# Two attention layers on one core: x read in blocks of 32 and turned by VectorE, with new orders of work

## The chip, the cores and the metric

One core of a Trainium2 chip runs the whole program, one launch. The metric is device microseconds of that core. Shown are the median of three runs and one execution taken by the profiler. TensorE (PE in the profile) does the products, VectorE (DVE), ScalarE (ACT) and GpSimd (POOL) the work between them, SyncE (SP) issues the DMAs. Each engine takes its instructions in the order in which they were written, and waits on semaphores.

## The reference

128 graphs of 128 nodes with 384 features go through two attention layers of 12 heads of 32, each with a residual and a layer norm. All arithmetic is f32.

```
# layer 0, for each graph
q, k, v = x @ Wq0.T, x @ Wk0.T, x @ Wv0.T + bv0
s  = q_h @ k_h.T * 384**-0.5 + 2 * adj          # rows that are all zero give p = 0
x1 = layernorm(x + concat(softmax(s) @ v_h) @ Wo0.T + bo0)
# layer 1
q, k, v = x1 @ Wq1 + bq1, x1 @ Wk1 + bk1, x1 @ Wv1 + bv1
s   = q_h @ k_h.T * 32**-0.5 + beta * adj, and -9e15 where adj <= 0
out = layernorm(x1 + concat(softmax(s) @ v_h))
```

## The kernel before

The graphs are taken in 64 pairs. Everything between x and the output stays in SBUF and PSUM. A product with f32 precision is split: each operand is kept as a high part (`_hi`, f32r) and a low part (`_lo`, the difference), and `split_product` adds three products, hi x hi, hi x lo and lo x hi, over three chunks of 128 features: nine matmuls. A `project_qk` makes one 128-feature chunk of q or k for both graphs of a pair (nine matmuls of 256 columns; six such calls a layer), `project_v` and `project_out0` a graph's v or output projection (nine of 384 columns). `scores` and `attend` are 24 small matmuls each, `transpose_x`, `transpose_x1` and `transpose_out1` three transposes of 128 x 128 through PSUM.

`iterations` runs the body of each engine for n = -2 to 68, the middle of it as a hardware loop of two bodies a turn. In a body, `n` is the current pair and `m1`, `m2`, `p1`, `p2` the pairs before and after it: the body is a software pipeline, in which layer 0 of the current pair, layer 1 of pairs two to five back and the first projections of the next stand side by side. The order of the calls in a body is written out by hand for each engine, and the five orders are independent: what an engine finds at its head it waits for.

`r_bank` is a ring of four PSUM banks for all results but the scores. Who uses which bank follows from the list `RING_USERS`, in TensorE's order; `BANK` is the place in it modulo four. `s_bank` are four banks for the scores of both layers.

The way of x before: `load_x` (line 231) brings a graph as 128 rows of 384 into `x_in`, two buffers; `transpose_x` (line 333) transposes it on TensorE into a bank of the ring; `high_xT` (line 499, ScalarE) copies it to `xT_hi`; `low_xT` (line 720, VectorE, through `low_part`, line 715) subtracts that from the bank into `xT_lo`. `residual0` (line 865, GpSimd) adds `bo` to `x_in` into `x_bo`, which `add_residual0` (line 657, VectorE) adds to the output projection.

The probabilities of layer 0: `negate` (line 678, VectorE) takes the scores out of PSUM with their maxima, `exps` (line 574, ScalarE) the exponentials. Meanwhile `fold_scores0` (line 892, GpSimd) adds the negated scores in halves, which `abs_max` (line 739, VectorE) sums, to find rows that are all zero. `inverse_sums0` (line 775, VectorE) makes the factor of each row and head, `normalise0` (line 919, GpSimd) multiplies, `flip_probs` (line 700, VectorE) transposes in blocks of 32 into `flip0`, and `spread_probs` (line 283, SyncE) brings the blocks to their places in `probT` with four DMAs. The fold's scratch lies in `flip0` as well, and it says so by a wait:

```
fold_a = flip0[:, 0:H * N // 2].rearrange("p (h k) -> p h k", h=H)
...
pool.wait_ge(probT_loaded[0], q.count(16 * NB, g, 0))
```

Other work of GpSimd is `make_bias1` (line 877: three steps that make the mask and bias of layer 1), `inverse_std` (line 848: three small steps of a layer norm), `late_x1` (line 903) and `residual1` (line 912).

At the start SyncE loads x of pair 0, then the weights by `load_weights` (line 262), one DMA each, the biases and the adjacency; GpSimd's first step behind its constants is line 951, which needs the biases bq and bk. `high_weights` (ScalarE) and `low_weights` split the weights.

Of the kernel before, what the change touches and what calls it, by code (L numbers as in the profile page):

```python
# [20 lines left out]
F32 = mybir.dt.float32  # L21
# [10 lines left out]
NB = N // HD  # L32
PAIRS = NG // 2
# [20 lines left out]
RING_USERS = ["g0_4", "v1_1", "v0_1", "x1t0", "g0_5", "x1t1", "xt0", "pv0_0",  # L54
              "pv1_0", "xt1", "g1_0", "g1_1", "ot_0", "g0_0", "g1_2", "g1_3",
              "g1_4", "wo_0", "pv1_1", "pv0_1", "g0_1", "g1_5", "g0_2", "g0_3",
              "ot_1", "wo_1", "v0_0", "v1_0"]
RING = 4
assert len(RING_USERS) % RING == 0
# [52 lines left out]
def build(nc, x, adj, wts, bv0, bo0, bq1, bk1, bv1, beta, out):  # L112

    with ExitStack() as ctx:
# [26 lines left out]
        x_in = [sb(f"x_in{b}", [P, 2, D]) for b in range(2)]  # L141
# [9 lines left out]

        xT_hi, xT_lo = sb("xT_hi", [P, C, G2], F32R), sb("xT_lo", [P, C, G2], F32R)
# [33 lines left out]
        x_loaded, adj0_loaded, adj1_loaded = sems("x_loaded"), sems("adj0_loaded"), sem("adj1_loaded")  # L186
# [8 lines left out]
        xt_done, x1t_done = sem("xt_done"), sem("x1t_done")  # L195
# [34 lines left out]
        def _(sp):  # L230
            def load_x(q):
                if q.valid():
                    b = q.parity

                    sp.wait_ge(xt_done, q.plus(-2).count(1, 1, 1))
                    sp.wait_ge(x_bo_done, q.plus(-2).count(1, 1, 1))
                    for g in range(2):
                        sp.dma_start(x_in[b][:, g, :], x[bass.ds(2 * q.index() + g, 1)].rearrange("g (j a) d -> a j (g d)", j=NB)
                                     ).then_inc(x_loaded[b], 16)
# [25 lines left out]


            load_x(Pair(0, 0))
            load_weights(WQ0)
            load_weights(WK0)
            for layer, b_ in enumerate((bv0, bv1)):  # L270
                sp.dma_start(bv_row[layer][:], b_.partition_broadcast(P)).then_inc(bv_loaded, 16)
            load_weights(WV0)
# [21 lines left out]
            def body(r, off):  # L294
                n = Pair(r, off)
                m5, m4, m3, m2, m1, p1, p2 = (n.plus(-5), n.plus(-4), n.plus(-3), n.plus(-2), n.plus(-1), n.plus(1), n.plus(2))

                spread_probs(1, m4, 1)
                if not is_peeled(r, off, -1):
                    load_adj0(p1)  # L300
                spread_probs(0, m1, 1)
                load_adj1(m2)
                store(m5, 1)
                spread_probs(1, m3, 0)
                spread_probs(0, n, 0)
                if not is_peeled(r, off, -2):
                    load_x(p2)
                store(m4, 0)
# [8 lines left out]
        def _(pe):  # L317

            read = [(xt_lo_done, 0, 0, 0, 0)] * 4
# [12 lines left out]

            def transpose_x(q, g, r):
                if q.valid():
                    pe.wait_ge(*last_read(read, BANK[f"xt{g}"], r))
                    read[BANK[f"xt{g}"]] = (xt_lo_done, q.off, 1, g, 1)
                    pe.wait_ge(x_loaded[q.parity], q.loads(2))
                    for c in range(C):
                        mm = pe.transpose(ring(f"xt{g}")[:, c * P:(c + 1) * P],  # L339
                                          x_in[q.parity][:, g, c * P:(c + 1) * P], ident[:])  # L340
                    mm.then_inc(xt_done, 1)
# [110 lines left out]
            def body(r, off):  # L452
                n = Pair(r, off)
                m4, m3, m2, m1, p1, p2 = (n.plus(-4), n.plus(-3), n.plus(-2), n.plus(-1), n.plus(1), n.plus(2))

                scores(0, n, 0, r)
                transpose_x(p1, 1, r)
                project_qk(1, m2, 0, r)
                project_qk(1, m2, 1, r)
# [33 lines left out]
        def _(act):  # L493
# [97 lines left out]
            def body(r, off):  # L591
# [6 lines left out]
                if is_peeled(r, off, -1):  # L598
                    high_weights(WO0)
# [383 lines left out]
```

## Time and profile before

| | |
|---|---|
| median of three runs | 2124.54 us (2122.32 to 2125.64) |
| profiled execution | 2125.58 us, span 2123.8 us from the first to the last instruction |
| mean granted clock of TensorE | 0.985 |
| busy share of the span | TensorE 96%, ScalarE 89%, VectorE 85%, GpSimd 77% |
| data moved by DMA | 273 MB on SyncE's queue in 225,360 packets |

Busy is the time in which an engine had an instruction running. "Idle before, releaser" is the time it stood still ahead of an instruction, and the line whose semaphore ended that. TensorE's matmuls overlap, so their spacing, not their length, is what one costs.

### The profile page before, as it was taken

The numbers are of one execution on the slowest core, as the hardware profiler recorded it, in microseconds if no ns is written. First come the engines' busy times: TensorE is split into PE (matmuls) and PEld (weight loads), VectorE is DVE, ScalarE is ACT, GpSimd is POOL, SyncE is SP. The second block draws the span as 40 slices with busy tenths as digits, with TensorE's granted clock in tenths as the row PEclk, the third lists the DMA queues.
The fourth block names the chain that finished last, engine by engine and source line by source line (L and its number), as shares of the span: only waits on it lengthen the run. The fifth ranks groups of instructions, "written<-read, shape, count | busy, mean of one in ns | idle before, by whom it ended". The sixth has DMA issues, their size and how long they took to land.

```text
span 2123.8 us, 86803 instructions
## 1 busy us (share of the span) xinstructions
PE 2046.2 (96%) x23808; PEld 1923.4 (91%) x23808; DVE 1814.6 (85%) x8324; ACT 1888.1 (89%) x7816; POOL 1643.1 (77%) x2187
## 2 busy tenths in 40 slices
PE   5799999999999999999999999999999999999984
PEld 5799999999999999999999999999999999999973
DVE  3578888888988988888988988988989888888875
ACT  4489999999999999999999999999999999999975
POOL 2667877888877878878878888888888888787774
PEclk9899999999999999999999999999999999999997
DMA  4245555555555555555555555555555555555554
GB/s 134 58 101 136 135 130 136 132 128 135 132 136 127 133 139 124 136 135 128 138 134 130 137 133 130 141 131 126 139 132 129 134 132 136 127 132 139 118 122 107
DMA packets 225439, 274.19 MB, mean 129 GB/s; under 512 B 25681, under 2 KB 225361, under 8 KB 225361
## 3 DMA queue, kind: packets, MB, share of 16 engines
q1 hardware_dynamic: 225360, 273.26, 53.5%
q8 instruction: 36, 0.59, 0.1%
q14 instruction: 43, 0.34, 0.1%
HBM read 46.67 MB, written 25.17 MB: 34 GB/s over the span
## 4 chain that ended last, share of the span: by engine, by line
PE 87%; POOL 4%; issue 3%; DMA 3%; SPq 2%; DVE 1%; ACT 0%; POOLq 0%; DVEq 0%
PE r_bank L356 22%; PE r_bank L357 21%; PE r_bank L358 21%; PE s_bank L407 10%; PE r_bank L423 8%; DMA prob0T<-flip 2%; PE r_bank L339 2%; PE r_bank L349 2%; PE r_bank L435 2%; SPq L291 1%; POOL prob L924 1%; POOL flip L897 1%; DVE flip L711 1%; POOL w_lo L845 0%; DMA stage<-in_L_gnn_Wv_dram 0%
## 5 line engine op out<-in xcount | busy, mean ns | idle before, releaser
L586 ACT ACTIVATE prob<-neg_s,heads 128x128 f32<-128x128 f32 x3072 | 1191.1, 394 | 18.7 <-DVE flip L711 11.1
L586 ACT ACTIVATION_READ_ACCUMULATOR prob<-neg_s,heads 128x1 f32 x3072 | 594.2, 193 | 0.0
L924 POOL TENSOR_TENSOR prob<-prob,heads 128x512 f32<-128x512 f32 x384 | 389.2, 1042 | 98.7 <-DVE heads L783 98.7
L897 POOL TENSOR_TENSOR flip<-neg_s 128x768 f32<-128x768 f32 x128 | 235.8, 1842 | 186.6 <-DMA prob0T<-flip 171.3
L356 PE MATMUL r_bank<-xT_hi,w_hi 128*128 128x256 f32 x1152 | 357.9, 311 | 14.6 <-DVE xT_lo L717 13.6
L695 DVE CUSTOM_DVE_ANT_0 neg_s<-s_bank,bias 128x128 f32<-128x128 f32 x1536 | 333.5, 286 | 20.6 <-PE s_bank L407 18.9
L695 DVE CUSTOM_DVE_ANT_0 neg_s<-s_bank,adj 128x128 f32<-128x128 f32 x1536 | 333.8, 286 | 2.3 <-PE s_bank L407 1.6
L356 PE MATMUL r_bank<-x1T_hi,w_hi 128*128 128x256 f32 x1152 | 330.8, 287 | 3.8 <-DVE x1T_lo L717 3.8
L358 PE MATMUL r_bank<-xT_hi,w_lo 128*128 128x256 f32 x1152 | 327.9, 285 | 0.0
L357 PE MATMUL r_bank<-xT_lo,w_hi 128*128 128x256 f32 x1152 | 327.9, 285 | 0.0
L357 PE MATMUL r_bank<-x1T_lo,w_hi 128*128 128x256 f32 x1152 | 325.0, 282 | 0.0
L358 PE MATMUL r_bank<-x1T_hi,w_lo 128*128 128x256 f32 x1152 | 324.8, 282 | 0.0
L356 PEld LDWEIGHTS r_bank<-xT_hi,w_hi 128*128 128x128 f32 x1152 | 219.4, 190 | 43.6 <-DVE xT_lo L717 14.6
L695 DVE DVE_READ_ACCUMULATOR2_ANT heads<- 128x1 f32 x3072 | 255.7, 83 | 0.1
L711 DVE STREAM_TRANSPOSE flip<-prob 128x1536 f32<-128x1536 f32 x128 | 227.4, 1777 | 20.6 <-POOL prob L924 19.3
L711 DVE STREAM_TRANSPOSE stage<-prob 128x1536 f32<-128x1536 f32 x128 | 225.4, 1761 | 7.5 <-DMA prob1T<-stage 7.5
L356 PEld LDWEIGHTS r_bank<-x1T_hi,w_hi 128*128 128x128 f32 x1152 | 217.7, 189 | 5.3 <-issue 5.1
L357 PEld LDWEIGHTS r_bank<-xT_lo,w_hi 128*128 128x128 f32 x1152 | 220.8, 192 | 0.0
L358 PEld LDWEIGHTS r_bank<-xT_hi,w_lo 128*128 128x128 f32 x1152 | 220.3, 191 | 0.0
L357 PEld LDWEIGHTS r_bank<-x1T_lo,w_hi 128*128 128x128 f32 x1152 | 218.0, 189 | 0.0
L358 PEld LDWEIGHTS r_bank<-x1T_hi,w_lo 128*128 128x128 f32 x1152 | 217.7, 189 | 0.0
L858 POOL TENSOR_TENSOR norm<-norm,neg_half 128x1 f32<-128x1 f32 x256 | 144.0, 563 | 21.3
(85 smaller groups left out, 5493.6 us busy)
## 6 DMA issues: line engine op xcount, KB each, us to landing
prob0T<-flip SPq DMA_DIRECT2D x512, 192.0 KB, 3.6
prob1T<-stage SPq DMA_DIRECT2D x512, 192.0 KB, 3.6
x_in<-in_x_dram SPq DMA_DIRECT2D x128, 192.0 KB, 3.3
out_dram<-y SPq DMA_DIRECT2D x128, 192.0 KB, 2.3
adj<-in_adj_dram SPq DMA_DIRECT2D x256, 64.0 KB, 2.7
prob<-in_L_gnn_Wq_dram SPq DMA_DIRECT2D x1, 576.0 KB, 5.6
prob0T<-in_L_gnn_Wk_dram SPq DMA_DIRECT2D x1, 576.0 KB, 6.5
stage<-in_L_gnn_Wv_dram SPq DMA_DIRECT2D x1, 576.0 KB, 7.6
```

Of the source, the lines that this page charges most:

```text
L339: mm = pe.transpose(ring(f"xt{g}")[:, c * P:(c + 1) * P], x_in[q.parity][:, g, c * P:(c + 1) * P], ident[:])
L356: pe.matmul(dst, a_hi(c), b_hi(c), start=(c == 0), stop=False)
L357: pe.matmul(dst, a_hi(c), b_lo(c), start=False, stop=False)
L358: mm = pe.matmul(dst, a_lo(c), b_hi(c), start=False, stop=(c == C - 1))
L407: mm = pe.matmul(s_bank[j][:, c * N:(c + 1) * N], qT[layer][q.parity][rows, c, m], kT[layer][q.parity][rows, c, m], start=True, stop=True)
L423: mm = pe.matmul(ring(name)[HD * j:HD * (j + 1), c * N:(c + 1) * N], v[layer][q.parity][:, g, f], probT[layer][:, :, HC * c + j, :], start ...
L586: act.activation(prob[layer][:, h, :], neg_s[layer][:, h, :], ACT.Exp, bias=neg_max[layer][:, h:h + 1], scale=-1.0, accum_out=row_sum[laye ...
L695: dve.tensor_tensor_reduce(neg_s[layer][:, h, :], s_bank[b][:, (h // HC) * N:(h // HC + 1) * N], (adj0, bias1)[layer][q.parity][:, g, :], ...
L711: dve.transpose(flip[layer].rearrange("p (j h b) -> p h j b", j=NB, h=H), prob[layer][:].rearrange("p h (j a) -> p h j a", j=NB)).then_inc ...
L858: pool.tensor_tensor(rstd[layer][g][:], var_eps[layer][g][:], neg_half[:], ALU.pow).then_inc(rstd_steps[layer], 1)
L897: pool.tensor_tensor(fold_a, neg_s[0][:, :, 0:N // 2], neg_s[0][:, :, N // 2:N], ALU.add).then_inc(fold_steps, 1)
L924: pool.tensor_tensor(prob[0][:, hs, :], prob[0][:, hs, :], inv_sum0[:, hs].unsqueeze(2).to_broadcast([P, HC, N]), ALU.mult).then_inc(probn ...
```

## The change

x is read twice. `load_q` (SyncE) reads both graphs of a pair with four DMAs into `x_q`, a single buffer: partitions 32 i to 32 i + 31 take features 96 i to 96 i + 95 of the rows, 32 rows to a block, so its contiguous pieces are 96 features, 384 bytes. `flip_x` (VectorE) transposes `x_q` in blocks of 32 x 32 into `xT`; row 32 i + b of chunk c is then feature 96 i + 32 c + b. The weights that meet it (WQ0, WK0, WV0) are loaded in the same order of features by `load_rows`, four DMAs each, those of WQ0 and WK0 from ScalarE's queue. `high_xT` (ScalarE) reads `xT` in place of a PSUM bank, and `low_xT` is GpSimd's now; both read `xT` in the order of the nodes that the columns of `xT_hi` have, a step of 32 elements within runs of four. `load_x` reads x once more, straight into `x_bo`, where `residual0` adds `bo` in place. The six transposes of a pair and their two users of the ring are gone; the list has 26 names, no longer a multiple of four. All five orders of calls are new, and `load_q`, `load_adj0` and `flip_x` work two pairs ahead.

```
+            def load_q(q):
+                if q.valid():
+                    sp.wait_ge(xflip_done, q.count(1, 0, 0))
+                    for i in range(NB):
+                        sp.dma_start(x_q[HD * i:HD * (i + 1), :, :],
+                                     x[bass.ds(2 * q.index(), 2)].rearrange("g (j a) d -> a (g j) d", j=NB)[:, :, QD * i:QD * (i + 1)]
+                                     ).then_inc(xq_loaded, 16)
             def load_x(q):
-                    sp.wait_ge(xt_done, q.plus(-2).count(1, 1, 1))
-                    sp.wait_ge(x_bo_done, q.plus(-2).count(1, 1, 1))
+                    sp.wait_ge(y0_done, q.plus(-2).count(1, 1, 1))
...
+            load_q(Pair(0, 0))
+            load_rows(WV0)
...
+                if not is_peeled(r, off, -2):
+                    load_q(p2)
                 spread_probs(0, m1, 1)
                 store(m5, 1)
                 spread_probs(1, m3, 0)
+                if not is_peeled(r, off, -2):
+                    load_adj0(p2)
+                store(m4, 0)
                 spread_probs(0, n, 0)
+                load_adj1(m1)
+                load_x(n)
+                spread_probs(1, m3, 1)
...
-            def transpose_x(q, g, r):
...
             def high_xT(q, g):
-                    act.wait_ge(xt_done, q.count(1, g, 1))
+                    act.wait_ge(xflip_done, q.count(1, g, 1))
...
+                    act.activation(xT_hi[:, :, g * N:(g + 1) * N].rearrange("p c (a j) -> p c a j", j=NB), rows_xT(g), ACT.Copy).then_inc(xt_hi_done, 1)
...
+            def flip_x(q, g):
+                if q.valid():
+                    dve.wait_ge(xq_loaded, q.count(8 * NB, 1, 8 * NB))
+                    dve.wait_ge(xt_lo_done, q.plus(-1).count(1, g, 1))
+                    dve.transpose(xT[:, :, g * N:(g + 1) * N].rearrange("p c (j a) -> p c j a", j=NB),
+                                  x_q[:, g * NB:(g + 1) * NB, :].rearrange("p j (c b) -> p c j b", c=C)
+                                  ).then_inc(xflip_done, 1)
...
+            def low_xT(q, g):
+                if q.valid():
+                    pool.wait_ge(xt_hi_done, q.count(1, g, 1))
...
+                    pool.tensor_tensor(*(t.rearrange("p c (a j) -> p c a j", j=NB) if i != 1 else t.rearrange("p c (j a) -> p c a j", j=NB)
+                                        for i, t in enumerate((xT_lo[:, :, m], xT[:, :, m], xT_hi[:, :, m].bitcast(F32)))), ALU.subtract
+                                      ).then_inc(xt_lo_done, 1)
```

The new orders of the engines on which most turns (TensorE, VectorE, GpSimd; each call stands for one line of the body):

```
TensorE: project_qk(0, n, 4); scores(1, m3, 0); attend(1, m4, 0); transpose_x1(m2, 1); project_qk(0, n, 5);
  transpose_out1(m4, 0); attend(0, m1, 0); scores(0, n, 0); project_v(0, n, 1); project_qk(1, m2, 0);
  project_v(1, m2, 0); project_qk(1, m2, 1); project_out0(m1, 0); project_qk(1, m2, 2); project_qk(1, m2, 3);
  attend(1, m4, 1); scores(1, m3, 1); transpose_out1(m4, 1); project_qk(1, m2, 4); project_qk(1, m2, 5);
  attend(0, m1, 1); scores(0, n, 1); project_qk(0, p1, 0); project_out0(m1, 1); project_qk(0, p1, 1);
  project_qk(0, p1, 2); project_v(0, p1, 0); project_qk(0, p1, 3); transpose_x1(m1, 0); project_v(1, m2, 1)
VectorE: flip_probs(1, m3, 0); norm_input0(m1, 0); negate(1, m3, 1); flip_x(p2, 0); attention_out1(m4, 1);
  low_o0T(m1, 1); abs_max(n, 0); inverse_sums0(n, 0); negate(0, n, 1); add_residual0(m1, 1); flip_probs(0, n, 0);
  values_out0(p1, 0); norm_input1(m4, 1); norm_input0(m1, 1); flip_probs(1, m3, 1); inverse_sums1(m3, 1);
  low_x1T(m1, 0); negate(1, m2, 0); low_x1T(m1, 1); attention_out1(m3, 0); flip_x(p2, 1); low_o0T(n, 0);
  abs_max(n, 1); inverse_sums0(n, 1); negate(0, p1, 0); values_out0(p1, 1); flip_probs(0, n, 1);
  add_residual0(n, 0); norm_input1(m3, 0); inverse_sums1(m2, 0)
GpSimd: make_bias1(m2, 0); inverse_std(1, m4, 0); low_xT(p1, 0); low_xT(p1, 1); fold_scores0(n, 0);
  inverse_std(0, m1, 0); normalise0(n, 0); late_x1(m2, 0); residual1(m4, 1); make_bias1(m2, 1);
  inverse_std(0, m1, 1); inverse_std(1, m4, 1); late_x1(m2, 1); fold_scores0(n, 1); residual1(m3, 0);
  normalise0(n, 1); residual0(n)
```

## Rows read from the trace of the kernel before

**Rows 1.** Stretch, busy us: PE, PEld, DVE, ACT, POOL (instructions); clock, DMA share, GB/s.

```profile
400.00:1000.00 600.00, 600.00 (x7071) 567.14 (x7070) 537.75 (x2474) 556.95 (x2321) 485.29 (x646) 1.00 0.56 133
```

**Rows 2.** Timeline of TensorE, scores of layer 0 (start, length, instruction).

```profile
214.88 0.95 PE L407 MATMUL s_bank<-k0T,q0T 32*128 32x128 f32 x24
...
1921.41 1.26 PE L407 MATMUL s_bank<-k0T,q0T 32*128 32x128 f32 x24
```

**Rows 3.** Waits of GpSimd: in total, times, longest.

```profile
POOL flip L897 <- DMA prob0T<-flip: 171.3, 125, 8.2
```

**Rows 4.** Timeline of GpSimd, two turns; idle before and releaser in brackets.

```profile
1000.79 1.85 POOL L897 TENSOR_TENSOR flip<-neg_s 128x768 f32<-128x768 f32 x1 [1.30 <-DMA prob0T<-flip]
...
1005.24 3.04 POOL L924 TENSOR_TENSOR prob<-prob,heads 128x512 f32<-128x512 f32 x3 [1.51 <-DVE heads L783]
...
1016.79 1.84 POOL L897 TENSOR_TENSOR flip<-neg_s 128x768 f32<-128x768 f32 x1 [1.04 <-DMA prob0T<-flip]
...
1019.81 0.22 POOL L855 TENSOR_SCALAR norm<-norm 128x1 f32<-128x1 f32 x1
...
1021.12 3.04 POOL L924 TENSOR_TENSOR prob<-prob,heads 128x512 f32<-128x512 f32 x3
...
1025.22 0.66 POOL L885 TENSOR_SCALAR mask<-adj 128x128 f32<-128x128 f32 x1
...
1027.35 0.24 POOL L855 TENSOR_SCALAR norm<-norm 128x1 f32<-128x1 f32 x1
...
1032.19 1.86 POOL L897 TENSOR_TENSOR flip<-neg_s 128x768 f32<-128x768 f32 x1 [1.10 <-DMA prob0T<-flip]
```

**Rows 5.** Timeline of VectorE in the second of these turns.

```profile
1019.76 0.55 DVE L744 TENSOR_REDUCE heads<-flip 128x12 f32<-128x384 f32 x1 [0.45 <-POOL flip L900]
...
1024.28 1.78 DVE L711 STREAM_TRANSPOSE flip<-prob 128x1536 f32<-128x1536 f32 x1 [0.29 <-POOL prob L924]
```

**Rows 6.** Timeline of SyncE in that turn, the four issues of a spread.

```profile
1026.09 3.00 SPq L291 DMA_DIRECT2D prob0T<-flip  x4
```

**Rows 7.** Timeline of TensorE around the two transposes of x.

```profile
1004.02 0.49 PE L339 MATMUL r_bank<-ident,x_in 128*128 128x128 f32 x3
1004.44 0.86 PE L423 MATMUL r_bank<-prob0T,v 128*32 128x128 f32 x24
...
1006.77 0.55 PE L339 MATMUL r_bank<-ident,x_in 128*128 128x128 f32 x3
1007.07 0.36 PE L356 MATMUL r_bank<-x1T_hi,w_hi 128*128 128x256 f32 x1
1007.27 0.28 PE L357 MATMUL r_bank<-x1T_lo,w_hi 128*128 128x256 f32 x1
1007.39 0.28 PE L358 MATMUL r_bank<-x1T_hi,w_lo 128*128 128x256 f32 x1
```

**Rows 8.** Groups of instructions by shape: count, busy, mean ns, idle before.

```profile
L711 DVE STREAM_TRANSPOSE flip<-prob 128x1536 f32<-128x1536 f32 x128 | 227.4, 1777 | 20.6 <-POOL prob L924 19.3
...
L717 DVE TENSOR_TENSOR xT_lo<-r_bank,xT_hi 128x384 fp32r<-128x384 f32 x128 | 71.3, 558 | 35.0 <-ACT xT_hi L505 33.4
...
L565 ACT ACTIVATE x<-y,norm 128x384 f32<-128x384 f32 x128 | 90.2, 704 | 26.6 <-POOL norm L862 26.5
...
L505 ACT ACTIVATE xT_hi<-r_bank 128x384 fp32r<-128x384 f32 x128 | 62.5, 489 | 16.9 <-PE r_bank L339 14.6
...
L874 POOL TENSOR_TENSOR x_bo<-x_in,bo_row 128x384 f32<-128x384 f32 x128 | 127.4, 1017 | 0.0
```

**Rows 9.** DMA issues: count, KB each, median us to landing.

```profile
adj<-in_adj_dram SPq DMA_DIRECT2D x256, 64.0 KB, 2.7
```

**Rows 10.** Timelines of SyncE, TensorE and GpSimd at the start.

```profile
9.03 0.56 SPq L278 DMA_DIRECT2D bqk<-in_L_gnn_bk_dram  x1
...
15.54 0.55 PE L356 MATMUL r_bank<-xT_hi,w_hi 128*128 128x256 f32 x1 [9.15 <-DVE xT_lo L717]
...
16.96 0.26 POOL L951 TENSOR_SCALAR bq1s<-bqk 128x3 f32<-128x3 f32 x1 [15.30 <-DMA bqk<-in_L_gnn_bk_dram]
```

More of the change, by code:

```diff
@@ L139, in build @@
         neg_half = sb("neg_half", [P, 1])
-        x_in = [sb(f"x_in{b}", [P, 2, D]) for b in range(2)]
+        x_q = sb("x_q", [P, 2 * NB, QD])
         x_bo = [sb(f"x_bo{b}", [P, 2, D]) for b in range(2)]
@@ L264, in load_weights, with load_rows @@
                              ).then_inc(w_loaded[i], 16)
-            load_x(Pair(0, 0))
-            load_weights(WQ0)
-            load_weights(WK0)
+            def load_rows(i):
+                for k in range(NB):
+                    sp.dma_start(w_stage[i][HD * k:HD * (k + 1), :, :],
+                                 wts[i][QD * k:QD * (k + 1), :].rearrange("(c b) o -> b c o", c=C)).then_inc(w_loaded[i], 16)
+            load_q(Pair(0, 0))
+            load_rows(WV0)
             for layer, b_ in enumerate((bv0, bv1)):
                 sp.dma_start(bv_row[layer][:], b_.partition_broadcast(P)).then_inc(bv_loaded, 16)
-            load_weights(WV0)
             load_adj0(Pair(0, 0))
@@ L493, in _, with load_rows, rows_xT @@
         def _(act):
+            def load_rows(i):
+                for k in range(NB):
+                    act.dma_start(w_stage[i][HD * k:HD * (k + 1), :, :],
+                                  wts[i][QD * k:QD * (k + 1), :].rearrange("(c b) o -> b c o", c=C)).then_inc(w_loaded[i], 16)
+            load_rows(WQ0)
+            load_rows(WK0)
             def high_weights(*which):
                 for i in which:
-                    act.wait_ge(w_loaded[i], 16)
+                    act.wait_ge(w_loaded[i], 16 * (NB if i in (WV0, WQ0, WK0) else 1))
                     act.activation(w_hi[i][:], w_stage[i], ACT.Copy).then_inc(w_hi_done[i], 1)
+            def rows_xT(g):
+                return xT[:, :, g * N:(g + 1) * N].rearrange("p c (j a) -> p c a j", j=NB)
             def high_xT(q, g):
                 if q.valid():
-                    act.wait_ge(xt_done, q.count(1, g, 1))
+                    act.wait_ge(xflip_done, q.count(1, g, 1))
                     if g == 0:
@@ new lines, in body @@
+                qk_out(1, m1, 0, r)
+                exps(1, m2, 0, 6, 8)
+                values_out1(m1, 0)
+                exps(1, m2, 0, 8, 10)
+                high_xT(p2, 1)
+                if is_peeled(r, off, -2):
+                    high_weights(WO0)
+                exps(1, m2, 0, 10, 12)
+                exps(0, p1, 0, 0, 2)
+                qk_out(1, m1, 1, r)
+                exps(0, p1, 0, 2, 4)
+                qk_out(1, m1, 2, r)
+                qk_out(1, m1, 3, r)
+                out1T_out(m3, 1)
```

244 lines of the change are left out of this document (106 added, 138 removed).

## The prediction

> **What bounds the kernel now.** I read the page's busy shares first (the table above). They average over filling, steady state and draining, so next comes the steady state alone, the windows view from 400 to 1000 us [rows 1]: TensorE is busy 600.00 of 600.00 us, ScalarE 556.95, VectorE 537.75, GpSimd 485.29, at a granted clock of 1.00 (its level of 2.4 GHz). TensorE has no gap at all there. Third, the length of a pair: the first layer's scores of graph 12 start at 214.88 and those of graph 120 at 1921.41, 54 pairs later [rows 2], so a pair takes 1706.53 / 54 = 31.60 us. 64 pairs of that are 2022 us; the other 101 us of the 2123.8 us span are filling and draining.
>
> The fourth view is there because a full TensorE hides what is second. In the waits of GpSimd, the fold of layer 0 (line 897) waits 125 times for the transfer prob0T<-flip [rows 3]: nearly every one of 128. So there is a ring of work that is almost as long as TensorE's pair. flip0 is a single buffer and also the scratch of the fold: fold, abs_max, inverse, normalise, flip, four DMAs, landing, next fold. Two turns of it, one per graph, start at 1000.79, 1016.79 and 1032.19 [rows 4]: 16.00 + 15.40 = 31.40 us. The reader is to see in [rows 4 to 6] that the second turn has nothing slack in it: fold 1016.79, maximum of its sums 1019.76, normalise 1021.12 to 1024.16, flip 1024.28 to 1026.06, four DMAs issued 1026.09 to 1029.09, next fold 1032.19. The first turn is 0.6 us longer. Two turns at the shorter length are 30.80 us. The change touches no step of this ring but where its steps stand in the queues, so whatever TensorE is relieved of, a pair will not go below about 30.8.
>
> **The change part by part.**
>
> TensorE loses two triples of transposes per pair. In [rows 7] the first starts at 1004.02 and the next instruction at 1004.44, 0.42 us; the second runs from 1006.77 to 1007.07, 0.30 us. Together 0.72 us a pair, which are on the path that sets the end. The order of what is left is new too. TensorE's body had seven runs of short matmuls (transposes, scores, attend) between the wide products; the new one has five. Behind a short run the first wide product holds the next one back: 1007.07 to 1007.27, and 0.12 us from there to the third [rows 7], so two runs fewer could give 0.2 more; but attend now stands right behind a projection twice, which the trace of before has nowhere, and that may take back as much as 0.2. I take 31.60 - 0.72 = 30.88 us for TensorE, ends 30.7 and 31.1.
>
> VectorE loses low_xT, 558 ns twice [rows 8], and gains flip_x, a stream transpose of 384 elements per partition. The trace has it only at 1536 elements, 1777 ns. A quarter of that is 0.44, the lower end; the upper end is the 0.56 that VectorE needs today for a pass over 384 elements. I take 0.55, for an instruction has a fixed part: VectorE's work stays as it is, 28.3 us a pair (537.75 / 600 of 31.60).
>
> ScalarE's high_xT reads SBUF instead of PSUM, in a permuted order. Lower end the 489 ns of today, upper end the 704 ns of a ScalarE pass over 384 elements in SBUF with its own scale and bias [rows 8]. It is nearest to the first, a plain copy, so 0.5. ScalarE is at 29.3 us a pair and stays there, at most 29.8: no bound, but 95% of the new pair.
>
> GpSimd gains low_xT twice a pair, a subtraction of 384 elements from SBUF. GpSimd's waits for others in the two turns of [rows 4] are 1.51, 1.04 and 1.10 us, so it is occupied 31.40 - 3.65 = 27.75 us a pair. The nearest row has the same size and contiguous operands: 1017 ns [rows 8], 1.10 with the gap to the next. The new one reads one of three operands with a step of 32 elements, inner runs of four. No GpSimd row has such a step; the other end is the fold of 768 elements, 1.84 us, as if each element cost double. I take 1.1, since two of the three streams stay as they are. GpSimd: 27.75 + 2.2 = 29.95, and 0.3 that it must still wait between its fold and normalise (that gap, filled by inverse_std today, is 1019.81 to 1021.12, 1.3 us, and in one turn the new order puts residual1 there, 1.0 us). 30.25 us: under TensorE, but with hardly a gap. At 1.84 us it is 31.9 with the gaps.
>
> The Trainium skill's page GPSIMD Engine Reference, section Performance pitfalls for Q7 kernels, speaks against this move: a read from SBUF whose step is over 8 bytes costs about 2.9 cycles an element instead of 1.9. By that low_xT would be an estimated 1.34 us and GpSimd 30.9 us a pair, level with TensorE; no run here shows it yet.
>
> The ring's window for GpSimd counts as well. From the end of normalise to the next fold the flip and its transfer take 1024.16 to 1032.19, 8.0 us. In one turn GpSimd now has residual0, make_bias1, inverse_std and both low_xT there: 2.0 + 2.1 + 1.3 + 2.2 = 7.6 us (residual0 is twice line 874 [rows 8]; bias 1025.22 to 1027.35 and inverse 1019.81 to 1021.12 [rows 4]). In the other late_x1 twice, residual1, make_bias1 and inverse_std twice: about 7.9. Both fit, by 0.4 and 0.1 us; the ring stays near 30.8.
>
> SyncE issues four more DMAs a pair (x_q) and reads x twice. Four flip issues take 3.0 us [rows 6], so four x_q issues about 3 us of a queue that now spends 24 issues on 31.6 us. The x_q DMAs stand ahead of the spread of the second graph's probabilities, released by flip_x of the pair before, which stands six steps ahead of that spread's flip in VectorE's order. What must land after them is on the ring. 96 KB in rows of 384 bytes each: nearest are the 64 KB adjacency blocks in rows of 512 bytes, 2.7 us [rows 9], and the flip's 192 KB, whose last part lands 3.1 us after the four issues end [rows 4, 6]. They should be gone before the spread starts; each microsecond that they are not lengthens one turn by as much.
>
> The start gets longer. Before, TensorE's products begin at 15.54, and GpSimd has no part in that; its own first work waits until 16.96 for bk, issued at 9.03 [rows 10]. Now low_xT of pair 0 stands behind that wait. As the 17th DMA of SyncE's queue in place of the 14th (four x_q for two x, four WV0 for one, less WQ0 and WK0, which go to ScalarE's queue), at 0.6 us an issue, bk comes at 17 to 19, then two low_xT, so TensorE starts at 19 to 22: 3.5 to 6.5 us later, I take 5. The draining follows the same chain; I cost it at nothing, ends -4 and +4.
>
> **The sum.** The pair is the longest of TensorE 30.88, the ring 30.80, GpSimd 30.25; as three in-order queues that meet within 0.6 us will not mesh without loss I add 0.1, an estimate: 31.0. About 60 pairs run at that rate, since the first few, which the ring sets, do not: 60 x (31.60 - 31.00) = 36 us. Less 5 at the start: the span becomes 2123.8 - 31 = 2092.8. The profiled execution took 2125.58, 1.8 beyond its span, so 2094.6; the median of the runs shown, 2124.54, is 1.0 below the profiled one. I forecast 2094 us. Below 0.2%, 4.2 us, a measurement of this kernel can't tell a difference.
>
> **The rivals.**
>
> *GpSimd becomes the bound.* If low_xT costs 1.84 us, GpSimd's pair is 31.9: 60 x 0.3 + 5 = 23 us more, 2147. For it: the only unmeasured access pattern falls on the engine that the ring passes through. Against it: two of three streams are contiguous. The point where it decides: 60 x (31.60 - P) = 5 gives P = 31.52, that is 27.75 + 0.3 + 2c = 31.52, c = 1.74 us with the gap, about 1.65 in the row. This is the case on the slower side, chance 0.14.
>
> *The ring holds the pair.* The extra transfers (1024 rows of x_q a pair) make the spread land later, or VectorE comes late to abs_max or flip because something ahead of it in the new order waits for TensorE. Half a microsecond a turn on one of the two turns gives 31.4 instead of 30.8: 60 x 0.2 - 5 = 7 us gained, 2117; a whole one gives 31.8, 2141. For it: the first turn is already 0.6 us longer than the second, so the queues do cost it something today. Against it: the spreads land some microseconds before attend wants them. Chance 0.17 for 2109 to 2121, of which a fifth lies within the 0.2%; another 0.06 for no change at all.
>
> The Trainium skill's page DMA: Bandwidth & Descriptors, section Specifications, is on this rival's side: under 512 bytes a transfer does not run at line rate, for the engine reads, modifies and writes. The shortest data rows of before are the adjacency's 512 bytes, so the trace can't say what 384 cost.
>
> *The change doesn't do what it says*, in that TensorE's idle time grows by what the transposes gave back: then the pair stays at 31.6 and the start's 5 us make 2129. It is in the chances of no change and slower, 0.03.
>
> **How the numbers follow.** The forecast, 2078 to 2108, has 0.60. Faster by over 0.2% is that and most of the ring's case: 0.74. Within 0.2%: 0.10. Slower: 0.16. The range that leaves two in ten out runs from 2076 (the pair at the ring's 30.8, start +3.5, draining -4) to 2122.
>
> **What would show it.** Right: the scores' spacing at about 31.0 us with TensorE still full; VectorE's stream transpose of 384 at about 0.55 us; low_xT near 1.1; waits of the fold for prob0T<-flip much smaller, since GpSimd comes to it late. Wrong: low_xT at 1.6 or more and GpSimd without any wait; attend (line 423) waiting for prob0T; spreads that land over 4.5 us after issue; TensorE's first product after 22 us.

## The result: slower, 2145.57 us

The changed kernel takes 2145.57 us (median of 4 runs, 2144.28 to 2147.01) against 2123.56 for the kernel before (4 runs, 2122.32 to 2125.64): a ratio of 1.0107, with a 95% interval of 1.0091 to 1.0122. The forecast was 2094, with a range from 2076 to 2122. The profiled execution of the changed kernel took 2144.28 us with a span of 2142.0.

### The profile after

The steady state of the kernel after, in the same windows view as [rows 1]:

```profile
400.00:1000.00 600.00, 598.67 (x6940) 559.17 (x6938) 536.34 (x2469) 566.87 (x2314) 527.05 (x684) 1.00 0.59 145
```

By its share TensorE is as full as before, at the same granted clock of 1.00, but it gets through 6940 matmuls in place of 7071. Six transposes fewer in each of the 19 pairs of that stretch explain 6 x 19 = 114 of the 131; the rest fits pairs that come a little more slowly. GpSimd is up by 42 us and ScalarE by 10; VectorE is where it was.

The length of a pair comes from TensorE's timeline. The first two of these rows are the first and the last graph of the kernel before, start, length and instruction of the scores of layer 0 (graphs 12 and 120 are in [rows 2]):

```profile
27.32 0.95 PE L407 MATMUL s_bank<-k0T,q0T 32*128 32x128 f32 x24
...
2034.31 1.67 PE L407 MATMUL s_bank<-k0T,q0T 32*128 32x128 f32 x24
```

The kernel after, graphs 0, 12, 120 and 127:

```profile
32.34 0.95 PE L407 MATMUL s_bank<-k0T,q0T 32*128 32x128 f32 x24 [0.47 <-ACT k0T L547]
...
214.97 0.95 PE L407 MATMUL s_bank<-k0T,q0T 32*128 32x128 f32 x24
...
1928.93 1.26 PE L407 MATMUL s_bank<-k0T,q0T 32*128 32x128 f32 x24
...
2045.64 0.95 PE L407 MATMUL s_bank<-k0T,q0T 32*128 32x128 f32 x24
```

The subtraction tells where the 18.2 us of span went. The start costs 5.0 (27.32 to 32.34), but filling gives it back: graph 12 starts at 214.97, as before. The 54 pairs from graph 12 to graph 120 take 1713.96 us, 31.74 a pair in place of 31.60: 7.4 us. The last graphs, 120 to 127, take 116.7 in place of 112.9: 3.8 us. From there to the end it is 96.4 in place of 89.5: 6.9 us. So the pair, which was to become 0.6 us shorter, is 0.14 longer.

The groups of the parts that are new or moved (count, busy, mean ns, idle before), answering to [rows 8]:

```profile
L917 POOL TENSOR_TENSOR flip<-neg_s 128x768 f32<-128x768 f32 x128 | 233.6, 1825 | 76.5 <-DMA prob0T<-flip 75.5
...
L908 POOL TENSOR_TENSOR xT_lo<-xT,xT_hi 128x384 fp32r<-128x384 f32 x128 | 153.3, 1220 | 16.1 <-ACT xT_hi L514 16.1
L514 ACT ACTIVATE xT_hi<-xT 128x384 fp32r<-128x384 f32 x128 | 118.5, 928 | 12.0 <-PE r_bank L358 8.2 <-DVE xT L733 2.1 <-issue 1.3
L733 DVE STREAM_TRANSPOSE xT<-x_q 128x384 f32<-128x384 f32 x128 | 73.0, 571 | 15.3 <-POOL xT_lo L908 9.8 <-DMA x_q<-in_x_dram 5.5
```

flip_x takes 571 ns (0.55 was taken), low_xT 1220 (1.1), high_xT 928 (0.5, with 0.704 as the upper end).

GpSimd's waits (in total, times, longest) answer to [rows 3]:

```profile
POOL flip L917 <- DMA prob0T<-flip: 75.5, 115, 8.3
```

The total is less than half of 171.3, which looks like the forecast, but the count says otherwise: in 115 of 128 turns the fold still waits for the spread of the graph before. GpSimd comes to it later, because low_xT now fills the time; the spread still lands last. Here are three turns in GpSimd's timeline, in the place of [rows 4]:

```profile
1008.22 1.84 POOL L917 TENSOR_TENSOR flip<-neg_s 128x768 f32<-128x768 f32 x1
...
1021.20 2.39 POOL L908 TENSOR_TENSOR xT_lo<-xT,xT_hi 128x384 fp32r<-128x384 f32 x2
1023.97 1.82 POOL L917 TENSOR_TENSOR flip<-neg_s 128x768 f32<-128x768 f32 x1 [0.39 <-DMA prob0T<-flip]
...
1039.70 1.83 POOL L917 TENSOR_TENSOR flip<-neg_s 128x768 f32<-128x768 f32 x1 [0.37 <-DMA prob0T<-flip]
...
1055.99 1.82 POOL L917 TENSOR_TENSOR flip<-neg_s 128x768 f32<-128x768 f32 x1 [0.91 <-DMA prob0T<-flip]
```

The turns take 15.75, 15.73 and 16.29 us, and in each the wait of the fold is what closes it. One step of the ring starts late for a reason that can be seen. VectorE's flip of the turn that begins at 1023.97, and SyncE's queue behind it:

```profile
1031.43 1.78 DVE L720 STREAM_TRANSPOSE flip<-prob 128x1536 f32<-128x1536 f32 x1
```

```profile
1031.21 1.33 SPq L252 DMA_DIRECT2D adj<-in_adj_dram  x2
1032.75 0.65 SPq L265 DMA_DIRECT2D out_dram<-y  x1
1033.57 3.04 SPq L300 DMA_DIRECT2D prob0T<-flip  x4
```

The flip ends at 1033.21. SyncE is then still issuing the store that stands ahead of the spread (to 1033.40), and the first of the four DMAs goes out at 1033.57, 0.36 us late. Averaged over the turns of graphs 20 to 115, a turn from fold to fold takes 15.79 us for the first graph of a pair and 15.91 for the second, 31.70 together; in the kernel before 15.51 and 16.07, 31.58. There is one fold per graph, so these sums are the length of a pair whatever sets it. What tells more is each step inside a turn, and SyncE's delay behind the flip above all: it averages 0.03 us for the first graph and 0.59 for the second in the kernel before, and 0.39 and 0.03 in the kernel after. The long turn of [rows 4], which begins at 1000.79, shows where the 0.59 came from. VectorE and SyncE of the kernel before, in that turn:

```profile
1008.40 1.78 DVE L711 STREAM_TRANSPOSE flip<-prob 128x1536 f32<-128x1536 f32 x1
```

```profile
1009.29 1.33 SPq L246 DMA_DIRECT2D adj<-in_adj_dram  x2
1010.72 3.05 SPq L291 DMA_DIRECT2D prob0T<-flip  x4
```

The flip ends at 1010.18, but the adjacency's load stands ahead of the spread and is being issued until 1010.62. The new order moved this load, with a store, ahead of the other graph's spread, and the delay moved with it.

That leaves a question: how can TensorE wait for anything if it is busy 598.67 of 600 us? Its timeline around two scores (after each, the first wide product that follows):

```profile
1009.79 1.08 PE L407 MATMUL s_bank<-k0T,q0T 32*128 32x128 f32 x24
1010.80 0.45 PE L356 MATMUL r_bank<-w_hi,xT_hi 128*128 128x384 f32 x1
...
1025.10 0.95 PE L407 MATMUL s_bank<-k0T,q0T 32*128 32x128 f32 x24
1026.04 0.38 PE L356 MATMUL r_bank<-xT_hi,w_hi 128*128 128x256 f32 x1
```

The first step takes 1.01 us and shows no gap, because the scores are drawn longer. In other pairs the same step takes 0.88. If for each of the 30 stretches of a pair, from the start of one block of products to the start of the next, the 5th percentile over 48 pairs of the steady state is taken, they add up to 30.99 us; the means add up to 31.70. Taking the 5th percentile as the work and the rest as waits, the kernel before has 31.40 us of work in a pair and 0.2 of waits. So TensorE's own work is 0.4 us shorter than before, and its waits grew from 0.2 to 0.7 us. These stand at four places: after the scores of each graph of layer 0 (0.20 and 0.25 us a pair on average), and around the projection of the attention's output (0.12 and 0.07).

### The profile page after: what moved, and what is told of

The parts are those of the page before. It is cut to its first block, busy times and chain, and to the rows that moved or that the text cites. A ratio compares the mean times of both kernels' runs of the same rounds, so it can differ in the third digit from the quotient of the medians.

```text
span 2142.0 us, 86733 instructions
## 1 busy us (share of the span) xinstructions
PE 2045.4 (95%) x23424; PEld 1905.7 (89%) x23424; DVE 1818.7 (85%) x8324; ACT 1928.7 (90%) x7816; POOL 1789.1 (84%) x2315
## 4 chain that ended last, share of the span: by engine, by line
PE 62%; POOL 17%; issue 9%; DVE 4%; DMA 4%; SPq 2%; ACT 1%; POOLq 1%; DVEq 0%; ACTq 0%
PE r_bank L356 16%; PE r_bank L358 15%; PE r_bank L357 15%; PE s_bank L407 8%; PE r_bank L423 6%; POOL flip L917 4%; DMA prob0T<-flip 4%; POOL prob L944 2%; POOL norm L868 2%; PE r_bank L435 2%; PE r_bank L349 2%; SPq L300 1%; POOL x_late L929 1%; DVE neg_s L704 1%; POOL flip L920 1%
## 5 line engine op out<-in xcount | busy, mean ns | idle before, releaser
L356 PE MATMUL r_bank<-xT_hi,w_hi 128*128 128x256 f32 x1152 | 339.4, 295 | 29.8 <-POOL xT_lo L908 23.7
L908 POOL TENSOR_TENSOR xT_lo<-xT,xT_hi 128x384 fp32r<-128x384 f32 x128 | 153.3, 1220 | 16.1 <-ACT xT_hi L514 16.1
```

Of the source, the lines that this page charges most:

```text
L356: pe.matmul(dst, a_hi(c), b_hi(c), start=(c == 0), stop=False)
L908: pool.tensor_tensor(*(t.rearrange("p c (a j) -> p c a j", j=NB) if i != 1 else t.rearrange("p c (j a) -> p c a j", j=NB) for i, t in enum ...
```

## The experiments

Four theories of where the gain went: **A**, the ring of fold, maximum, normalise, flip, spread and next fold is as long as a pair and holds it; **B**, ScalarE and GpSimd are too full with high_xT at 928 and low_xT at 1220 ns; **C**, the traffic of x_q delays the spreads; **D**, VectorE's new order makes TensorE wait for banks whatever the ring does.

**own_scratch: the ring opened.** The fold's scratch leaves flip0 for a third of stage that is free by then, so the fold waits for the maximum of the graph before instead of the landing of its spread.

```
-        fold_a = flip0[:, 0:H * N // 2].rearrange("p (h k) -> p h k", h=H)
-        fold_b = flip0[:, H * N // 2:H * N * 3 // 4].rearrange("p (h k) -> p h k", h=H)
+        fold_a = stage[:, H * N:H * N * 3 // 2].rearrange("p (h k) -> p h k", h=H)
+        fold_b = fold_a[:, :, 0:N // 4]
...
-                    pool.wait_ge(probT_loaded[0], q.count(16 * NB, g, 0))
+                    pool.wait_ge(absmax_steps, q.count(2, g, 0))
...
```

> The changed kernel with the scratch of the fold moved out of flip0 into the free third of stage, so that the fold no longer waits for the landing of the spread before it. Theory A, the ring (fold, maximum, normalise, flip, four DMAs, landing, fold) sets the pair of 31.74 us: the ring is open now, TensorE becomes the bound at its stall-free 31.0 us, 60 x 0.7 = 42 us less than 2145, about 2103, and the hidden stalls of TensorE behind scores go. Theory B, ScalarE (94% busy, high_xT at 0.93 us) with GpSimd is simply full and each call waits for another: the pair stays above 31.5, 2130 to 2146. Theory C, the extra DMA traffic of x_q: the spreads still land late, but nothing but attend waits for them: also about 2105, so this run alone does not tell A from C.

2113.70 us, 0.995 of before [0.9933, 0.9966]; the pair is 31.30. The fold no longer waits for a DMA at all. 32 us come back by one change of place of a scratch buffer: theory A has most of it. It is 11 us short of the 2103 that A gave, for one wait of TensorE is left: in each of 48 pairs of the steady state project_qk(0, p1, 0) starts 0.13 us after the end of VectorE's attention_out1.

**contig: ScalarE and GpSimd relieved, the ring closed.** flip_x writes its result with a step, so that high_xT and low_xT read contiguous rows.

```
...
-                    dve.transpose(xT[:, :, g * N:(g + 1) * N].rearrange("p c (j a) -> p c j a", j=NB),
+                    dve.transpose(xT[:, :, g * N:(g + 1) * N].rearrange("p c (a j) -> p c j a", j=NB),
...
```

> The changed kernel with flip_x writing its blocks into the final order of the columns (a step of 4 elements on VectorE's side), so that high_xT and low_xT read and write contiguously. Theory A (ring): high_xT falls to about 0.5 us and low_xT to 1.02, but the ring keeps its length: pair 31.5 to 31.7, 2132 to 2145. Theory B (ScalarE and GpSimd full): 0.8 us a pair off ScalarE and 0.4 off GpSimd give the pair 31.1 or so, about 2107. Theory C: no change, 2145. flip_x itself may take longer than 0.57 us with the step.

2145.64 us, 1.0101 [1.0084, 1.0118]; the pair is 31.78. The groups (count, busy, mean ns, idle before) and the steady state of this kernel:

```profile
L908 POOL TENSOR_TENSOR xT_lo<-xT,xT_hi 128x384 fp32r<-128x384 f32 x128 | 126.6, 1011 | 15.3 <-ACT xT_hi L514 15.3
L733 DVE STREAM_TRANSPOSE xT<-x_q 128x384 f32<-128x384 f32 x128 | 113.4, 887 | 12.4 <-POOL xT_lo L908 7.5 <-DMA x_q<-in_x_dram 4.9
L514 ACT ACTIVATE xT_hi<-xT 128x384 fp32r<-128x384 f32 x128 | 66.3, 519 | 13.5 <-PE r_bank L358 8.4 <-DVE xT L733 2.6 <-issue 1.3
```

```profile
400.00:1000.00 600.00, 594.10 (x6935) 555.25 (x6934) 541.03 (x2458) 556.54 (x2308) 519.06 (x682) 1.00 0.59 145
```

high_xT and low_xT become as cheap as forecast, ScalarE is back at the 557 us of [rows 1], and the pair doesn't move. But flip_x now takes 887 ns in place of 571 on VectorE, so this run alone would leave theory B a way out. own_scratch closes it: there ScalarE and GpSimd have the same work as in the kernel after, and the pair is 31.30. Theory B falls.

**xq_short: the traffic taken away.** After the first pair each x_q DMA reads one of its eight blocks.

```
+                    blocks = slice(0, 2 * NB if is_peeled(q.r, q.off, 0) else 1)
...
-                        sp.dma_start(x_q[HD * i:HD * (i + 1), :, :],
+                        sp.dma_start(x_q[HD * i:HD * (i + 1), blocks, :],
```

> The changed kernel with the four x_q DMAs of each pair behind the first reading one of eight blocks, so 128 rows of 384 bytes a pair instead of 1024 (what is left out is seven eighths of the read of x for layer 0's products; the steps and waits stay). Theory C: the spreads land 0.2 to 0.3 us earlier, two turns a pair, pair about 31.2, about 2113. Theory A: a little of that, 31.5 to 31.7, 2130 to 2143. Theory B: 2143 to 2147.

2143.87 us, 1.0099 [1.0082, 1.0116]. The DMA share of the stretch goes from 0.59 to 0.54, the turns stay at 15.81 and 15.89, and the spreads land no earlier: the last part 3.98 and 4.35 us after its issue began, in place of 3.98 and 4.37. Theory C falls, as far as the bytes go; the four issues are still there.

**before_scratch: the ring opened in the kernel before.** The same edit in the other kernel.

```
...
-                    pool.wait_ge(probT_loaded[0], q.count(16 * NB, g, 0))
+                    pool.wait_ge(absmax_steps, q.count(2, g, 0))
...
```

> The kernel before with the same own scratch of the fold, as a control. Theory A says that TensorE, which had no gap in steady state, is the bound there and the ring (31.40 of 31.60 us) is not: the pair stays at 31.55 to 31.60, only the filling, where the ring ruled for some eight graphs, gets shorter: 2095 to 2122. If the ring had set the pair of the kernel before too, its pair would fall below 31.4.

2118.58 us, 0.9976 [0.9966, 0.9985]. The pair stays at 31.60 (1706.4 us for the 54); the gain lies in filling, where graph 12 starts at 209.5 in place of 214.9, and in draining. So in the kernel before TensorE, with its own order, holds the 31.60 with the ring open as well, and the closed ring, though its fold waits in 125 of 128 turns, isn't what sets the pair. How much shorter than 31.60 that ring would turn by itself, this run doesn't show.

**sp_order: one known delay of the ring taken out.** The spread of the first graph goes ahead of the adjacency's load and the store in SyncE's order; the ring stays closed.

```
                 spread_probs(1, m3, 0)
+                spread_probs(0, n, 0)
                 if not is_peeled(r, off, -2):
                     load_adj0(p2)
                 store(m4, 0)
-                spread_probs(0, n, 0)
```

> The changed kernel with one move in SyncE's order: the spread of the first graph's probabilities stands ahead of load_adj0 and the store, which in the changed kernel delay its first issue by 0.39 us behind the flip. The ring stays closed. Theory A (the ring sets the pair): the pair falls by about that, 31.74 to 31.35, 54 pairs of it are 21 us, about 2122. Theory B (the ring was only one of several that meet; what is taken out of one place turns up as a wait at the next of its steps): the 0.39 us goes into later waits, pair 31.6 to 31.75, 2138 to 2146.

2130.71 us, 1.0029 [1.0019, 1.0039]; the pair is 31.48. VectorE's flip and SyncE's queue in a turn of this kernel:

```profile
1026.77 1.78 DVE L720 STREAM_TRANSPOSE flip<-prob 128x1536 f32<-128x1536 f32 x1
```

```profile
1028.58 3.03 SPq L300 DMA_DIRECT2D prob0T<-flip  x4
1031.88 1.41 SPq L252 DMA_DIRECT2D adj<-in_adj_dram  x2
```

The flip ends at 1028.55 and the spread goes out at 1028.58. Of the 0.36 us that left the first graph's turn the pair got back 0.26, which is as a ring that sets the pair would have it, but for 0.1. GpSimd's waits show where the 0.1 went:

```profile
POOL flip L917 <- DMA prob0T<-flip: 60.2, 72, 7.9
```

The fold waits in 72 turns, no longer in 115: at the end of the first graph's turn GpSimd now comes to it behind the landing, 3.10 us after the end of the last issue in place of 3.00. There GpSimd's own order ends the turn. (Theory B of the expectation is that of several bounds that meet, not the B from above; a little of it is true.)

**dve_first: only VectorE's order.** attention_out1, which frees a bank for TensorE, goes ahead of flip_x; the ring stays closed.

```
-                flip_x(p2, 0)
                 attention_out1(m4, 1)
+                flip_x(p2, 0)
```

> The changed kernel, ring closed, with one swap in VectorE's order: attention_out1(m4, 1) ahead of flip_x(p2, 0). TensorE's project_qk(0, p1, 0) reuses the bank that attention_out1 reads, and stalls there about 0.25 us a pair. Theory A (the ring sets the pair of 31.74): the stall is only where TensorE's waiting for the ring shows, so the pair stays within 0.1 us, 2139 to 2147. Theory D (this wait of TensorE on VectorE is the bound): the flip's 0.5 us go from the path, pair about 31.3, 2115 to 2122.

2145.06 us, 1.0092 [1.0075, 1.0109], a pair of 31.79. The wait after the scores of the second graph shrinks (from 1.16 to 1.06 us on average to the next block) and that after the first graph's grows (from 1.07 to 1.17): the sum is the ring's. Theory D falls as the cause.

**scratch_dve: both.** The ring opened and attention_out1 first.

```
+        fold_a = stage[:, H * N:H * N * 3 // 2].rearrange("p (h k) -> p h k", h=H)
...
-                flip_x(p2, 0)
                 attention_out1(m4, 1)
+                flip_x(p2, 0)
...
```

> The same swap on the changed kernel with the fold's own scratch (pair 31.30, where the stall ahead of project_qk(0, p1, 0) is the one left). Theory A with D behind it: ring open and attention_out1 0.5 us earlier, TensorE reaches its stall-free 31.05: 54 x 0.25 = 13 us less than 2114, about 2100. If the stall is a wait for low_xT on GpSimd instead, no change: 2112 to 2116.

2109.03 us, 0.9924 [0.9908, 0.9941], a pair of 31.20. It is the best of all kernels here, and beats the kernel before by 16 us; theory A with D behind it had 2100. Its steady state, and the scores of two graphs with what follows:

```profile
400.00:1000.00 600.00, 600.00 (x7010) 563.93 (x7004) 537.31 (x2502) 579.26 (x2345) 534.78 (x692) 1.00 0.60 147
```

```profile
1007.35 0.95 PE L407 MATMUL s_bank<-k0T,q0T 32*128 32x128 f32 x24
1008.23 0.39 PE L356 MATMUL r_bank<-xT_hi,w_hi 128*128 128x256 f32 x1
...
1023.19 0.95 PE L407 MATMUL s_bank<-k0T,q0T 32*128 32x128 f32 x24
1024.07 0.44 PE L356 MATMUL r_bank<-w_hi,xT_hi 128*128 128x384 f32 x1
```

In both the step is 0.88 us, where the rows of the kernel after have 0.94 behind the second graph's scores and 1.01 behind the first's. In every second pair the step behind the second graph's is still longer, 1.24 us. With the ring open the order of VectorE is worth 0.1 us a pair; with the ring closed it was worth nothing.

**scratch_dve_sp: sp_order on top.** The spread of the first graph ahead of load and store, ring open.

```
...
                 spread_probs(1, m3, 0)
+                spread_probs(0, n, 0)
...
```

> As scratch_dve, with the spread of the first graph ahead of load_adj0 and the store in SyncE's order as well. With the ring open SyncE's 0.39 us are on no ring; both theories: as scratch_dve within 4 us. If it gains as much as it did with the ring closed (15 us), the spread's landing is still on the path, by way of flip or attend.

2109.76 us, 0.9929 [0.9912, 0.9946], a pair of 31.21. What gave 0.26 us a pair with the ring closed gives nothing when it is open. That is the strongest evidence that the ring passed SyncE's delay on to TensorE.

**contig_scratch: the contiguous reads with the ring open.**

```
+        fold_a = stage[:, H * N:H * N * 3 // 2].rearrange("p (h k) -> p h k", h=H)
...
+                    dve.transpose(xT[:, :, g * N:(g + 1) * N].rearrange("p c (a j) -> p c j a", j=NB),
...
```

> The changed kernel with the fold's own scratch and the contiguous high_xT and low_xT together. With the ring open the pair was 31.30, TensorE 31.05 without stalls, ScalarE 96% busy. Theory A1 (behind the ring, ScalarE is next): 0.8 us less of ScalarE brings the pair to TensorE's 31.05, about 2100. Theory A2 (what is left is TensorE's one stall ahead of project_qk(0, p1, 0), which waits for VectorE's attention_out1): flip_x takes 0.89 in place of 0.57 us on VectorE, so the stall grows and the pair is 31.3 to 31.5, 2113 to 2125.

2127.09 us, 1.0011 [1.0001, 1.002], a pair of 31.54, which is 0.24 longer than own_scratch, though ScalarE and GpSimd do less. TensorE's waits (in total, times, longest) name what is late:

```profile
PE r_bank L356 <- DVE y L771: 16.1, 54, 0.4
```

flip_x at 887 ns stands ahead of attention_out1 (L771) on VectorE, and the bank that this frees comes later: project_qk(0, p1, 0) starts 0.13 us after the end of attention_out1 in each of 48 pairs, as in own_scratch, and its step behind the scores is 1.42 us in place of 1.17, which is all of the 0.24. The 0.3 us on VectorE at that place are worth more than the 0.8 on ScalarE and 0.4 on GpSimd that they save. The time lies 2 us above what theory A2 had.

**old_order, old_order_scratch and old28: the new way of x in the old orders.** To tell whether the orders took the gain, x_q, flip_x and high_xT were put into the five bodies of the kernel before, without transpose_x. In the first two low_xT stays on VectorE and the list of banks loses xt0 and xt1; old_order_scratch opens the ring as well. old28 has the ring open, keeps the old list of 28 and has low_xT on GpSimd.

VectorE's body of before, and TensorE's:

```
             def body(r, off):
...
+                flip_x(p1, 1)
                 low_x1T(m2, 1)
...
                 values_out0(p1, 1)
+                flip_x(p2, 0)
                 low_x1T(m1, 0)
...
-                transpose_x(p1, 1, r)
...
-                transpose_x(p2, 0, r)
```

GpSimd's body in old28:

```
+                low_xT(p1, 1)
                 late_x1(m3, 0)
...
                 normalise0(n, 1)
+                low_xT(p2, 0)
```

> The new way of x in the orders of the kernel before: transpose_x left out of TensorE's order, flip_x on VectorE where it is needed, low_xT on VectorE at its old places (reading xT in SBUF), load_q at the place of load_x and load_x one pair later, the ring list without its two names. So GpSimd has its old work. Theory A: TensorE loses 0.72 us a pair but the closed ring, 31.4 us in the kernel before, keeps the pair at 31.2 to 31.5: 2105 to 2122. If the new orders were needed for the change, some queue jams and the pair is over 31.6: 2125 or more.

> The same with the fold's own scratch. Theory A: the ring is open, TensorE has 30.9 us of work, VectorE 29.4, ScalarE 30.2: pair 30.9 to 31.2, and the filling gains as it did in the kernel before with own scratch: 2080 to 2100. If VectorE's 1.1 us more or the closer reuse of the ring's banks is what counts, 31.3 or more: over 2100.

> The new way of x in the orders of the kernel before once more, with the fold's own scratch, but with the list of 28 places kept (xt0 and xt1 stand for nothing, so no bank is reused closer than before) and low_xT on GpSimd at the two places where VectorE had it. In old_order the list of 26 names and VectorE's low_xT of 1.25 us were both changed. If the ring's list was the jam there, the waits for values_out0 and x1T_lo go and the pair is 31.0 to 31.8, 2090 to 2125; if the old orders have no room for low_xT ahead of project_qk(0, p1, 0), TensorE waits for xT_lo each pair, 32 us or more, over 2135.

2333.50 us (1.0974 [1.0955, 1.0992]), 2282.51 (1.0745 [1.0727, 1.0763]) and 2194.23 (1.0325 [1.0308, 1.0342]). All are far slower than before, by waits that the old orders have no room for. TensorE's waits in old_order:

```profile
PE r_bank L353 <- DVE v L788: 126.6, 63, 3.6
PE r_bank L353 <- DVE x1T_lo L721: 79.3, 61, 2.4
```

and in old28:

```profile
PE r_bank L356 <- POOL xT_lo L906: 117.4, 62, 21.5
```

In old_order VectorE frees TensorE's banks late (values_out0 and low_x1T), with a low_xT of 1248 ns in its queue in place of 558; whether that or the shorter list of banks does it, the two old_order runs don't separate. In old28 it is GpSimd's low_xT itself, once a pair by (117.4 - 21.5) / 61 = 1.6 us. So with the calls placed as here the new way of x doesn't fit into the old orders. These runs don't tell what part of the lost gain is due to the new orders; sp_order shows one such part, 15 us by SyncE's order alone.

## Why the prediction was wrong, step by step

**The step that failed** is the term "the ring 30.80" of the sum. It is twice the shorter turn, 15.40, and so it puts at nothing what the queues add to a turn. With the ring closed its two turns take 31.70 and the pair 31.74; with the ring open the same kernel takes 31.30. The sentence that a pair "will not go below about 30.8" stands unrefuted (the shortest pair of all runs is 31.20 on average): a floor was taken for the length. The first turn's extra 0.6 us was put down to "the queues", but not to a call in them. It was SyncE's delay behind the flip, 0.59 us on average, by the adjacency's load; in the new order the second graph's turn is rid of it (0.03), and the first graph's has 0.39 from the same load and a store. What the second graph's turn was rid of, 0.56 us, went for the most part to other steps of it: the factors are ready 0.20 us later behind the start of the maximum (1.41 in place of 1.21 us), and the last landing comes 4.37 us after its issue began in place of 4.00; why, no run isolates. The 125 waits in 128 turns of [rows 3] say that the loop was closed; they do not say whether the ring or TensorE set the pair, and neither does the mean of the turns. Opening the loop in both kernels does: nothing in the one (31.60), 0.44 us in the other.

**The rival that came true** is "The ring holds the pair". Its two prices, 31.4 and 31.8 us a pair, stand on both sides of the measured 31.74 (half a microsecond on 30.80 is 31.3, though, not 31.4). It had the right loop and "the queues do cost it something today", but looked for the delay in the transfers of x_q (xq_short: no) and on VectorE, and it is in SyncE's order. It had 0.23, none of it for its slower price, and should have had most of the chance. The rival of GpSimd gave 2147, nearly the time measured, but by another way: low_xT takes 1.22 us, not 1.65, and contig makes it 1.01 without any gain. That the number fits is luck.

**TensorE**: 30.88 was taken, 30.7 to 31.1 as ends; 30.99 is what its stretches add up to without waits, inside them. But the 31.60 that the 0.72 was taken from was not all work: by the same count it was 31.40, so TensorE is relieved of 0.4 us. The transposes did take 0.30 and 0.42; the four attends of a pair, in their new places, take 0.79 us each in place of 0.68 or 0.77, 0.27 together, where the prediction had allowed 0.2 and set as much against it. In scratch_dve the pair falls by 31.60 - 31.20 = 0.40: all of that relief, and 0.2 us of waits are left as before. So even an open ring doesn't bring the 31.0 of the sum.

**VectorE**: flip_x 0.571 for 0.55. Right, and the sum stays as it was (536 for 538 us). **ScalarE**: high_xT 928 ns for 500, outside its ends. This added 0.9 us a pair, and ScalarE's pair in scratch_dve is 579.26 / 600 x 31.20 = 30.1 us, so the miss was not the one that decided, as contig shows. **GpSimd**: 1.22 us for 1.1, between its ends. The Trainium skill's page GPSIMD Engine Reference, section Performance pitfalls for Q7 kernels, would have it at an estimated 1.34 for a read with a step over 8 bytes, 2.9 cycles an element instead of 1.9; the trace agrees in sign, but the step costs 1220 - 1011 = 209 ns here, where that estimate has 1.34 - 1.02 = 0.32 us (1017 ns without a step [rows 8]).

**SyncE**: x_q lands in 2.6 us, as the nearest rows had it, and reading an eighth of it changes nothing that a pair shows. The Trainium skill's page DMA: Bandwidth & Descriptors, section Specifications, cited for rows under 512 bytes, would have spoken for a loss; xq_short shows none. What the step on SyncE missed is that queue order, not bytes, lay on the ring: the adjacency load and the store stand ahead of the first spread.

**The start**: TensorE's first product at 21.18 us, inside 19 to 22, and for another reason than bk. WK0 now comes in four DMAs from ScalarE's queue and lands late. ScalarE's timeline at the start of the kernel after:

```profile
13.30 1.16 ACT L503 ACTIVATE w_hi<-prob0T 128x1152 fp32r<-128x1152 f32 x1 [4.45 <-DMA prob0T<-in_L_gnn_Wk_dram]
...
17.64 1.63 ACT L514 ACTIVATE xT_hi<-xT 128x384 fp32r<-128x384 f32 x2 [2.13 <-DVE xT L733]
```

VectorE's low parts of the weights follow it, flip_x comes after them (to 18.07), then high_xT and low_xT. GpSimd had done with bk at 17.65. And 5 us at the start were not 5 in the sum, for graph 12 starts when it did before. The ring sets part of the filling, as graph 12 starts 4.8 us earlier in own_scratch and 5.4 in before_scratch; what gave back the 5 us with the ring closed isn't shown.

**The draining** was costed at nothing, ends -4 and +4; it took 6.9 us more, and the seven graphs ahead of it 3.8. TensorE's waits after the last scores (in total, times, longest), first of the kernel before, then of the kernel after:

```profile
PE r_bank L423 <- DMA prob1T<-stage: 11.8, 3, 4.7
```

```profile
PE r_bank L423 <- DMA prob1T<-stage: 19.6, 4, 7.0
```

Attend of layer 1 waits 7.8 us more for its spread. own_scratch and scratch_dve show 19.3 too, so it isn't the ring. The last spread of layer 1 stands at the end of SyncE's new body, which would fit; that wasn't tried.

**Open.** Why scratch_dve stays 0.2 us above TensorE's 30.99 (one wait after the scores of the second graph is left, 0.18 us on average; it comes in every second pair, so once in a turn of the hardware loop, and its cause is not isolated); why the second graph's landing is later; the 3.8 us of the last graphs.

## What to carry to other kernels

Where a loop through several engines closes in nearly every turn (a wait that comes as many times as the loop turns, however short), don't take its shortest turn for its length, nor its mean turn for what it needs: the mean is the length of a pair whoever sets it. Go through a long turn step by step, find the call behind which each late step stood, and look where that call stands in the new order. Relieving the engine that looked full gave nothing here until that loop was opened. Opening it cost a place of its own for a scratch that shared its buffer with a transfer; a delay was then tested twice, with the loop closed and open, and one that counts only when it is closed was on the loop. In a full engine's timeline measure the step from block to block, not the busy share, take the best of it over many turns as the work and the rest as waits, and do so for both kernels: a best of one against a mean of the other makes the relief look larger than it is.

## What the runs showed of the hardware

- A step in what ScalarE reads from SBUF makes its copy 1.8 times as long: 384 elements take 928 ns with a step of 32 elements, 519 without (contig), 489 from a bank of PSUM [rows 8].
- VectorE's subtraction of 384 elements with one such operand takes 1248 ns in old_order, against 558 from PSUM [rows 8]; GpSimd's pays less, 1220 against 1011.
- VectorE's stream transpose of 384 elements takes 571 ns into contiguous rows and 887 when it writes each element four apart (contig).
- A TensorE that shows as busy for 598.67 of 600 us can still be waiting for 0.7 of 31.7 us in each pair: the records show it only as longer scores and later starts. In the kernel before it was 0.2 us of 31.6, at 600.00 of 600.
